# A two-layer decoder on one core: the work behind the context attention is spread, tile by tile, over the slots of its key-tile loop

## The reference, cut to what matters

```python
x = x + attn0(ln(x))      # 16 heads of 128, causal with a slope per head, over the 56 tokens of a batch
x = x + xattn0(ln(x), ctx)  # 16 heads of 16; K and V of the 1500 context rows; scores clipped to +-50, masked,
                            # softmax, divided once more by (sum + 1e-8), output projection, layer norm
x = x + ffn0(ln(x))       # quantise to 8 bits; gate and up (1024 wide) with ternary weights; silu(gate)*up;
                          # Hadamard transform; quantise again; down
x = x + attn1(ln(x))      # takes the 8 batches as the sequence: token s of batch b attends to token s of batches <= b
x = x + xattn1(ln(x), ctx)  # a decaying sum over the context, its mean added to ln(x), layer norm
x = x + ffn1(ln(x))       # 1024 wide; h rounded to steps of 0.1 and clipped, gelu, second product
```

## Time and profile before

| | |
|---|---|
| median of 3 runs | 623.88 us (622.65 to 624.21) |
| the profiled execution | 621.71 us |
| its span, first to last instruction | 618.8 us |
| mean granted TensorE clock | 0.905 |
| share of the span: PE, weight loads, DVE, ACT, POOL | 81%, 66%, 58%, 34%, 30% |

### The profile page before, as it was taken

How to read it: one execution, slowest core, us unless ns; L and a number is a source line. 1 busy time by engine, 2 the same in 40 slices (tenths; PEclk the granted TensorE clock), 3 DMA queues, 4 the chain that set the end, 5 groups by cost and what they waited for, 6 DMA issues and landing times.

```text
span 618.8 us, 15547 instructions
## 1 busy us (share of the span) xinstructions
PE 503.2 (81%) x6802; PEld 407.1 (66%) x6802; DVE 360.7 (58%) x630; ACT 211.1 (34%) x336; POOL 186.4 (30%) x83
## 2 busy tenths in 40 slices
PE   3994979999977999999999999998516766164296
PEld 2673767778765888888888888887413665143164
DVE  2236453443334686868777776764477843783652
ACT  1451323433335444444444444443102351101111
POOL 1004999500014435353525344420000001460100
PEclk9996989999989999999999999999758777656599
DMA  8720212221510111212121212100000000000001
GB/s 290 286 68 2 68 34 68 68 59 44 177 45 6 63 39 67 63 42 67 40 69 37 69 35 69 48 24 4 0 0 0 1 2 0 0 1 0 0 0 30
DMA packets 10685, 30.70 MB, mean 50 GB/s; under 512 B 1282, under 2 KB 4355, under 8 KB 9859
## 3 DMA queue, kind: packets, MB, share of 16 engines
q1 hardware_dynamic: 10434, 29.32, 14.6%
q0 software_dynamic: 192, 0.51, 0.3%
HBM read 29.36 MB, written 0.46 MB: 48 GB/s over the span
## 4 chain that ended last, share of the span: by engine, by line
PE 72%; DVE 18%; ACT 3%; issue 3%; POOL 2%; DMA 1%; DVEq 0%
PE psk L889 11%; PE psv L898 10%; PE psa L923 8%; PE psv L941 7%; PE psa L818 7%; PE psa L826 5%; PE psv L833 5%; PE psk L862 2%; PE psa L1088 2%; PE psk L1099 2%; PE psa L842 2%; DVE stats L487 2%; DVE xn L504 1%; DVE shared L541 1%; PE psk L853 1%
## 5 line engine op out<-in xcount | busy, mean ns | idle before, releaser
L630 DVE TENSOR_SCALAR shared<-shared,top 125x896 f32<-125x896 f32 x48 | 79.2, 1690 | 55.5 <-ACT shared L410 55.5
L276 POOL TENSOR_TENSOR cx<-ring,ones 128x1000 fp32r<-128x1000 f32 x24 | 45.0, 1876 | 119.1 <-DMA ring<-ctx_t_dram 119.1
L889 PE MATMUL psk<-cx,wkv 128*128 128x500 f32 x288 | 77.8, 406 | 0.0
L898 PEld LDWEIGHTS psv<-wkv,cx 128*125 128x125 f32 x552 | 71.1, 186 | 5.4 <-DVE vmem L594 2.0
L898 PE MATMUL psv<-wkv,cx 128*125 128x256 f32 x552 | 72.9, 281 | 0.6 <-DVE vmem L594 0.6
L410 ACT ACTIVATE shared<-psa 125x1792 f32<-125x1792 f32 x24 | 40.1, 1670 | 65.8 <-PE psa L923 65.8
L279 POOL TENSOR_TENSOR cx<-ring,cx 128x1000 fp32r<-128x1000 f32 x24 | 61.2, 2552 | 1.9
L410 ACT ACTIVATE smem<-psa 125x1792 f32<-125x1792 f32 x24 | 40.1, 1670 | 63.1 <-PE psa L923 63.1
L889 PEld LDWEIGHTS psk<-cx,wkv 128*128 128x128 f32 x288 | 50.5, 188 | 12.5
L923 PE MATMUL psa<-qb,kx 32*125 32x112 f32 x1536 | 54.7, 279 | 1.6 <-issue 1.6
L818 PE MATMUL psa<-xnT,whd 128*128 128x448 f32 x128 | 53.2, 561 | 0.0
(11 more groups left out here) (200 smaller groups left out, 824.7 us busy)
## 6 DMA issues: line engine op xcount, KB each, us to landing
ring<-ctx_t_dram SPq DMA_DIRECT2D x24, 500.0 KB, 3.4
whd<-heads_dram SPq DMA_DIRECT2D x16, 385.0 KB, 3.4
whd<-heads_dram SPq DMA_DIRECT2D x16, 129.0 KB, 2.2
wraw<-w_dram SPq DMA_DIRECT2D x2, 1024.0 KB, 6.0
mats_sb<-mats_dram SPq DMA_DIRECT2D x1, 1536.0 KB, 16.0
wraw<-gate_dram SPq DMA_DIRECT2D x1, 1024.0 KB, 10.1
wraw<-up_dram SPq DMA_DIRECT2D x1, 1024.0 KB, 12.2
wraw<-down_dram SPq DMA_DIRECT2D x1, 1024.0 KB, 13.9
```

The source lines that it names most:

```text
L276: nc.gpsimd.tensor_tensor(cx[HI][slot][:, :, :], ctxs[cs], ones[:, 0:1].unsqueeze(1).to_broadcast([P, DC, UT]), ALU.mult).then_inc(s_ch, 1)
L630: nc.vector.tensor_scalar(half, half, top[:, u // UPB, key:key + 1], 1.0 / ECLIP, ALU.min, ALU.max).then_inc(s_clip, 1)
L889: last = nc.tensor.matmul(PS[2][:, m, 0:UT], wkv[a][:, 0, c, m * P:(m + 1) * P], cx[b][u % 2][:, c, :], start=(a == b and c == 0), stop=(a ...
L898: last = nc.tensor.matmul(bank[0:CT, t * D:(t + 1) * D], cx[b][u % 2][:, c, a0:a0 + CT], wkv[a][:, 1, c, :], start=(a == b and c == 0), st ...
```

## The change

The loop over pairs becomes a loop over SLOTS = 73 slots. In slot s an engine first does its part of pair s (for s < 48), with the tail's steps at two places, `tail_early` and `tail_late`. The tail is cut by tile. Tile a runs its first half (context output, ffn0) in the twelve slots from 12(a+1), its second half (attn1, xattn1, ffn1) in the twelve after these. So tiles 0 to 2 run their first halves and tiles 0 and 1 their second halves inside the pairs; slots 48 to 59 hold the first half of tile 3 with the second half of tile 2, slots 60 to 71 the second half of tile 3, slot 72 its end. Each tile is stored by its own DMA.

PSUM is divided anew: four banks for scores, `kvb` for K and V of the loop in turn, `pvb` for the weighted values, `pst` (T0, T1) for the tail. So PE's order in a slot is scores, V, weighted values of the pair before, tail_early, K, tail_late, with a wait for ACT's move ahead of V and ahead of K. Moving V goes from DVE to ACT. DVE clips before it weighs.

1/sqrt(v + eps) is no longer Sqrt and reciprocal but Ln, Exp(-0.5 ...) on ACT, in the table set that the loop's exponentials use, and one Newton step on DVE. Silu and Gelu load their own tables in their slots and load the common set back. attn1 of a tile is on DVE alone (POOL takes no part): tile t has 2t+2 key batches. The constants made behind head 2 are spread over heads 2 to 6, the weight scale first. The hardware loops of heads and DMAs are unrolled. In the diff below the three loops over SLOTS are, in this order, those of ACT, DVE and PE.

```diff
-                nc.scalar.activation(std[:, :], veps[:, :], ACT.Sqrt).then_inc(s_std, 1)
+            def root(k, t=0, n=1):
+                act.wait_ge(s_var[k], t + 1)
+                nc.scalar.activation(lnv[:, a:a + n], nx[:, a:a + n], ACT.Ln, scale=-2.0).then_inc(s_act, 1)
...
+                nc.scalar.activation(y0[:, a:a + n], lnv[:, a:a + n], ACT.Exp, scale=-0.5).then_inc(s_rs[k], 1)
+            nc.scalar.preload_act_table_set("natural_log_exp_and_others")
...
+            def silu(t):
+                nc.scalar.preload_act_table(ACT.Silu)
+                act.wait_ge(s_gate, t + 1)
+                nc.scalar.activation(sil, both, ACT.Silu, scale=gu[:, t, 0:1]).then_inc(s_sil, 1)
+            def back():
+                nc.scalar.preload_act_table_set("natural_log_exp_and_others")
...
+            for s in range(SLOTS):
+                u, r = s // 2, s % 2
+                if s < PAIRS:
+                    act.wait_ge(s_qk, s + 1)
...
+                    nc.scalar.activation(ex[s % 2], psa[0:CT, :, 0:448], ACT.Exp, scale=0.25).then_inc(s_ex, 1)
+                    if u + 1 < B * UPB:
+                        move_vu(u + 1, r, kvb)
+                tail_early(s)
+                if u + 1 < B * UPB:
+                    move_k(u + 1, r, kvb)
+                tail_late(s)
...
+            def polish(k, t):
+                dve.wait_ge(s_rs[k], t + 1)
+                link(nc.vector.scalar_tensor_tensor(out=col(yt, k, t), in0=col(y0, k, t), scalar=col(y0, k, t), in1=col(nx, k, t),
+                                                    op0=ALU.mult, op1=ALU.mult))
+                link(nc.vector.scalar_tensor_tensor(out=col(rs, k, t), in0=col(yt, k, t), scalar=1.5, in1=col(y0, k, t),
+                                                    op0=ALU.add, op1=ALU.mult))
...
+            for s in range(SLOTS):
+                tail_early(s)
+                if s < PAIRS:
+                    clip(s)
+                    weigh(s // 2, s % 2)
+                if s % 6 == 0 and 0 < s <= PAIRS:
+                    take_raw(s // 6 - 1)
...
+                tail_late(s)
...
+            for s in range(SLOTS):
+                u, r = s // 2, s % 2
+                if s < PAIRS:
+                    scores(s)
+                    if u + 1 < B * UPB:
+                        pe.wait_ge(s_ke, s + 2)
+                        project_vu(u + 1, r, kvb)
+                if 0 < s <= PAIRS:
+                    weighted_values(s - 1)
+                tail_early(s)
                 if u + 1 < B * UPB:
...
+                    pe.wait_ge(s_vue, s + 3)
+                    project_k(u + 1, r, kvb)
+                tail_late(s)
```

More of the change, by code:

```diff
@@ L453, in _ @@
-            act.wait_ge(s_kvp, 1)
-            nc.scalar.activation(kv1.rearrange("p a b -> p (a b)"), PS[2][0:TT, :, :].rearrange("p a b -> p (a b)"), ACT.Copy).then_inc(s_qpe, 1)
-            act.wait_ge(s_sub, 1)
-            nc.scalar.activation(p1[:, :, :], s1[:, :, :], ACT.Exp, scale=0.25).then_inc(s_e1, 1)
-            for c in range(DC):
-                act.wait_ge(s_aT, c + 1)
-                nc.scalar.activation(xnT[:, c, :], PS[0][:, c, 0:TOK], ACT.Copy).then_inc(s_ae, 1)
-            root(5)
@@ new lines, in tail_late @@
+            def tail_late(s):
+                i, a, b = s % 12, s // 12 - 1, s // 12 - 2
+                if i == 0 and 0 <= b - 1 < NT:
+                    last_add(b - 1)
+                if 0 <= b < NT:
+                    if i == 1:
+                        score(b)
+                    if i == 2:
+                        attend(b)
+                    if i == 4:
+                        add_summary(b)
+                    if i == 8:
+                        clip_hidden(b, 0)
+                    if i == 10:
+                        clip_hidden(b, 1)
+                if 0 <= a < NT:
+                    if i == 2:
+                        centre_delta(a)
+                    if i == 3:
+                        quantise(a)
+                    if i == 6:
+                        times_up(a)
+                    if i == 7:
+                        butterfly(a, 1)
+                        butterfly(a, 2)
+                    if i == 9:
+                        quantise_hidden(a)
+                    if i == 11:
+                        add_down(a)
@@ L902, in _ @@
             pe.wait_ge(s_wkv, 1)
[L903 to L904 removed]
+            project_k(0, 0, kvb)
+            project_k(0, 1, pvb)
             for r in range(2):
```

1230 lines of the change are left out of this document (654 added, 576 removed).

## The result

The changed kernel takes 664.69 us (median of four runs, 663.83 to 665.32) where the kernel before took 623.90 in the same comparison (622.65 to 624.21): a ratio of 1.066, with a 95% interval of 1.064 to 1.068. It is slower by 41 us. The forecast was 600, with 625 as the upper end of its range. The profiled execution took 665.32 us, its span 663.1; the forecast's sum was made against the span, 595.8, so 67.3 us are to be found.

The account below looks back on a forecast made before the run. PE alone was taken to bound the pairs, and a chain that fills neither PE nor DVE the tail. Span 618.8 - 3 (heads) + 73 (pairs) - 93 (behind) = 595.8, with overheads 601; predicted 600 us, range 570 to 625.

Parts of the forecast that it names:

- Part 1: Heads: weight scale first removes most of PE's 7.72 us wait, scan and sum partly reach PE; -3 us, between -8 and +4.
- Part 2: Pairs: K and V share a bank, so PE waits about 0.9 us for K's move in odd slots; +23 us.
- Part 3: Pairs: 2.5 tiles of the tail's PE work come in, 35 to 50 us; taken +37.
- Part 4: Pairs: tail steps not ready in their slots (0, 2 to 3, 5) make waits; +11 us, between 0 and 22.
- part 5: Pairs: DVE's tail steps are held by POOL's split in even slots; +10 us, between 0 and 37.
- the 8 us of cover: Pairs: in about eight units tail_late work covers K's move; -8 us.
- The page on table loads: A skill page adds a drain of about 1.38 us per load, giving 623 us; the forecast stayed with 1.28 a load.
- Part 6: Behind the pairs: stretches of 56 and 40 us plus a 3.7 us store make 100 us, from 193; -93.
- DVE beside POOL decides: Rival, pairs: the lock costs 37 us, not 10, and held steps delay roots before exponentials; about 628 us, chance 0.17.
- The clock sags: Rival, pairs: PE busy 0.88 lowers the clock, 5% of 267 is 13 us; about 613 us, chance 0.06.
- The loads don't go away: Rival: Ln and Exp of each root bring their own tables, 61 us in line; over 650 us, chance 0.02.

Follow-up runs that it names:

- experiment 1: Changed kernel with four small VectorE operations (three for `top`, one scaling the weight means) moved ahead of the weight scale's release: 651.07 us.
- experiment 5: Changed kernel with the bounds, decay, scan and sum ahead of the heads and other small constants clear of GpSimd's quantisation: 629.25 us, 1.010 of the kernel before.
- experiment 2: Changed kernel without GpSimd's splits of context units from the third on (output not the reference's): 639.63 us.
- experiment 7: Changed kernel with K in the tail's bank T1, straight behind the scores, in slots 0 to 11: 654.25 us.
- experiment 4: Changed kernel with half of ffn1's products left out on TensorE (output not the reference's): 647.18 us.
- experiment 3: Changed kernel with Silu and Gelu replaced by Identity and without the sixteen table loads (output not the reference's): 657.99 us.
- experiment 10: Changed kernel with constants ahead of the heads, K in its own bank in slots 0 to 11 and unread products behind the pairs: 615.65 us, 0.988 of before.
- experiment 6: Kernel before with the same constants ahead of the heads and the last small ones behind head 1, tail unchanged: 609.49 us against 622.93, 0.979.

## Why the prediction was wrong, step by step

**Part 1, heads: -3 forecast, +22 measured.** The failed step is the sentence that PE's wait for the weight scale goes at no price but the scan's 3.6 and the sum's 2.0 us. The wait did go (7.72 to 0.64). But to release the weight scale first is also to start GpSimd's quantisation first, and every constant still to be made then runs beside it. The forecast knew the lock and priced it in the pairs; in the heads it priced one further wait of 4.77 us as the upper end and held the four small operations to be short. Experiments 1 and 5 show it: 15.9 and 34.6 us back. The Trainium skill (SBUF — State Buffer, Who interferes with whom), which the forecast used for the pairs, names the kinds as well: copies, casts and `tensor_scalar` can take the pair of ports shared with GpSimd, while `tensor_reduce` never does. The trace agrees in both directions: a cast of 96 elements took 5.03 us, a `tensor_scalar` of 3 elements 7.10, the reduction of 1500 its usual 1.70.

**Part 2, the bank: +23 forecast.** The mechanism is shown, the size nearly. Odd plain slots have the wait for K's move (0.77 us). The sum for a unit was 1.0 us and is 1.4, as even slots are longer too, 5.17 and not 4.97; twelve slots took 67.1 us where 5.4 each would be 65.

**Part 3, PE work: +37 forecast, +67.8 measured** (298.49 busy against 230.66). This is the largest error of a single term, and two steps failed in it. The first is the price of a product. The tail's own products, all that write `pst`, are busy 55.21 us in the pairs (a window from the first tail step to the end of the pairs, with only the instructions that write or read `pst`: PE, weight loads, DVE, ACT):

```profile
283.00:545.00 262.00, 55.21 (x338) 40.56 (x338) 14.72 (x26) 23.91 (x45) 0.95 0.11 34
```

Counted from start to start, so that overlaps with the loop's products fall out, they are some 51. That is 20 to 22 us a tile for two and a half tiles, where the sum had 15. The count by products took the 3.48 us of the earlier trace rows as those of eight products at the low clock, 0.22 each at the full one; but they are eight records and four products. At full clock the records of 256 columns start 0.215 us apart (16 in 3.62 us in experiment 2), so such an f32 product costs 0.43. The tile comes to 20 to 22 and not to twice the count's 14, as bf16 products and transposes leave one record. The forecast's other reckoning, 107.16 us at clock 0.74 being at most 79 at full clock, or 20 a tile, was nearly right; the sum took a value near the count instead.

The second is a term that the sum put at nothing: the loop's own products, which take the other 13 to 17 us. V now stands behind the scores and takes 1.68 us in place of 1.58 in each of 46 slots, 4.6 us; in experiment 7, where it stands behind K in slots 0 to 11, it takes 1.57 there. And by my sum of the groups, the stretches at half clock behind PE's waits lengthen V, K, scores and weighted values by about 7 us. The last few us weren't divided. Experiment 4 shows that the tail's part is paid for, experiment 2 that the half clock goes with the waits.

**Part 4, waits in the slots: +11 forecast**, and **part 5, the lock: +10 forecast, 25 measured** by experiment 2. PE stood idle 30.6 us of the pairs; the terms of parts 2, 4 and 5, with the 8 us of cover, made 36. So idle PE was no larger than forecast, but its parts were others: 14.1 us for K's move, 8.4 in four waits for V's move, 5.1 at `turn_context`, 2.1 at `normalise4`. The order in slot 0 and slot 5 was seen. What the sum lacked, and only the rival had, is that the lock starts these waits: it delays DVE's step, the step a root or PE itself, and the root an exponential. Taken away, the lock took those waits along, and what the sum didn't price at all, the half clock behind them (PE's busy time fell by 10 us of the 25). The kernel without table loads was 6.4 us faster in the pairs, where the forecast had 4.0, and 1.2 behind them; more than half of the 6.4 is not the loads' alone (experiment 3).

**The page on table loads.** The Trainium skill (ScalarE: Activation LUTs, What ACT_TABLE_LOAD costs) would have added a drain to each load. In slot 29 the V move ends at 407.25 and the load begins at 407.26; it ends at 408.54 and the silu begins at 408.56. No further time stands there, and the kernel without loads is 6.7 us faster, less than 1.28 for each. The row decides; the forecast was right to leave the drain out.

**Part 6, behind the pairs: 100 forecast, 118.1 measured.** The walk through the slots had the right form: a chain of DVE, ACT and PE in turn, with score and attend at 10.5 us in place of 10.8. The terms of PE in it were too small by the same reading of records as products. `project_hidden` was put at 3.48 us, twice, and takes 5.16 to 5.44; each hidden half and the Hadamard product takes 3.77. Experiment 4 takes 10.8 us out of this stage by halving ffn1's products, so PE's terms are paid for in full here. The first twelve slots took 64 us (545 to 609) where the walk had 56, the rest with the store 54 where it had 44; how these misses divide further was not settled.

**The rivals.** *DVE beside POOL decides* had the right mechanism and, in its price for the pairs, an end that the measurement approached (25 of 37). It was given 0.17 and 628 us, and it didn't reach to the heads, where the lock took the larger part. *The clock sags*: it did, to 0.96 in the pairs, though not evenly, as that rival had it, but to half in short stretches behind PE's waits; its price of 13 us was of the right order (7 us in the loop's products and 1.7 in `project_hidden`). *The loads don't go away*: they went; 17 loads were counted and none by a root. What was left out was any case in which parts 1 and 3 miss together.

**What the forecast would have been.** With the measured busy time of PE in part 3 (+31), the small operations in part 1 (+21) and 5.3 for 3.48 us twice in part 6 (+4) it is 656. The 9 us that are left don't tell how good the other terms were, since some were too high: the pairs missed by 24 us where part 3 alone missed by 31.

## What to carry to other kernels

When a step is moved earlier, ask what it releases, and then what else runs beside that: a 0.2 us VectorE copy or `tensor_scalar` linked into a row beside GpSimd instructions of 7 us costs 7 us each time. Put such constants where GpSimd is idle; here that alone made the kernel before 2% faster. And before work is moved under a stage that one engine bounds, hold the products of that engine in the code against its records in the trace, price one from rows whose clock you have looked up, and ask what each new wait does to the clock behind it: here the tail's PE work took 51 to 55 of the 74 us that spreading it won behind the pairs (experiment 10), and waits with what followed them took the rest.

## What the runs showed of the hardware

- A VectorE operation on 3 elements a partition took 7.10 us, and a cast on 96 elements 5.03, each until the GpSimd instruction beside it ended. Operations on one element a partition in the same place (L650, 0.14 us) and the scan with its two inputs (3.40) went through.
- The heads' scaling, a `tensor_tensor` with both inputs in SBUF, is held only at some times: it took 0.63 us from 52.98 inside a GpSimd instruction that ran from 48.45 to 55.62 (experiment 6), but 4.77 us from 79.70 beside one that had begun at 79.50; and that hold ended at 84.47, 2.1 us before the instruction did. What decides it was not settled.
- An f32 product leaves two records; an fp32r or bf16 product and a transpose leave one. In records of the same kind the time from start to start has two values: 0.215 and 0.427 us with 256 columns, 0.11 and 0.21 with 112 to 128. The group of 16 records L1211 took 3.62 us where all were of the first kind (experiment 2, slot 36; granted clock 1.00) and 5.3 to 5.6 where both stood in it (granted clock 0.64 to 0.68). So busy time does scale with the clock, record by record, but the mean clock of a long stretch doesn't price a group in it: the eight records of L1154 took 1.04 us at 555.21, inside a stretch of mean clock 0.61, because the granted clock was 1.00 just there.
- In the pairs of the changed kernel the granted clock was at half level within a microsecond behind PE's waits of 2.0 to 3.2 us, and V took 2.83 to 2.92 us there in place of 1.68. In experiment 4 such a wait (1.98 us before 456.68) was followed by full clock, so a wait of this length doesn't decide it alone; what does was not settled.
